# A normalised, quantised grouped convolution: TensorE's program as a loop of six trips over four images

## The chip, the cores and the metric

The kernel runs on one core of one Trainium2 chip. The metric is device time in microseconds (us) of one execution; the time before the change is a median of three runs. A profile is one execution, recorded instruction by instruction.

## The reference, cut to what matters

The input x is 32 images of 512 channels by 28 x 28 points (784), float32. Per image:

```python
x32 groups of 16 channels:  v = (x - mean) / sqrt(var + 1e-5)      # over 16 x 784 values
xg  = v as 4 groups of 128 channels, the groups rotated by one
xa  = round(clip((xg - lA) / (uA - lA), 0, 1) * 15) / 15
wq  = (round(clip((weight - lW) / (uW - lW), 0, 1) * 15) / 15 - 0.5) * 2
y   = einsum('bgihw,goi->bgohw', xa, wq)                           # 128 x 128 per group
y   = relu(y * inv + (beta - running_mean * inv))                  # inv = gamma / sqrt(running_var + 1e-5)
out = x + (y + v)
```

Every image is read once (1.6 MB) and written once (1.6 MB). Means and variances are of one image alone, so images can be worked on one behind the other.

## The kernel before, in words

All engines stream over the 32 images. Twelve image buffers (`images`, `RING`) hold an image as 128 channels of a partition group x 4 groups x 784. SyncE issues the loads (line 199); the load of image n waits until the store of image n-12 has landed. ScalarE issues 30 of the 32 stores (line 262), SyncE the last two (lines 203 and 212, the last one in four quarters).

Statistics of an image are taken five images ahead (`AHEAD`) by VectorE (`bn_stats`, line 460, summed in line 468 for a pair of images) and ScalarE (lines 236 and 242). TensorE averages them over 16 channels, for a pair u of images at a time: `average_means(u)` (lines 575 to 578), ScalarE copies the means (line 250), GpSimd makes the deviations (lines 375 to 382), `average_deviations(u)` (line 584) adds them up; then come a square root on ScalarE (line 257), a reciprocal on VectorE (line 492) and the coefficients on GpSimd (lines 398 to 406).

An image is then quantised to int16 `levels` (ScalarE line 270, mostly three groups; GpSimd line 424, the fourth), capped to bf16 `codes` by VectorE (`cap`, line 475), and multiplied by the weights, which are split in three bf16 parts: `multiply(n, g)` (lines 594 to 605) is six matmuls of 128 x 392, the last of which waits for GpSimd's in-place affine of the same group (line 413, semaphore `y_pool`). The sum goes to one of three PSUM sets of `prod`. VectorE's `finish(n, g)` (line 482) takes the set, applies the floor of the relu and adds it to the image; its semaphore `final` counts the sets that are free again and the groups that are done.

What sets the order: each engine's program is written out by hand and runs in that order; engines wait for each other by counting semaphores. TensorE's order for an odd image is multiply 0, 1, 2, `average_means`, multiply 3; for an even image `average_deviations`, multiply 0, 1, 2, 3. VectorE's for image n is finish 0, finish 1, cap(n+1), finish 2, half a group of statistics, finish 3, three more halves. With sets dealt in turn, `multiply` of the k-th group (k = 4n + g) waits for `finish` of group k-3:

```python
def multiply(n, g):
    k = G * n + g
    if g == 0:
        pe.wait_ge(capped, n + 1)
    if k >= SETS:
        pe.wait_ge(final, k - SETS + 1)
```

TensorE's program is unrolled: 999 matmuls with 999 weight loads.

Of the kernel before, what the change touches and what calls it, by code (L numbers as in the profile page):

```python
# [23 lines left out]
HELPED = 4  # L24
ACT_STORES = 30
SETS = 3
SUBSETS = 4
DMA = 16


def fused_norm_quantised_conv(nc, x, weight, limits, channel_params, out):

    B, C, H, W = x.shape
    G = CONV_GROUPS
    HW = H * W
    HALF = HW // 2
    PER_NORM = C // NORM_GROUPS
    COUNT = HW // SUBSETS
    PAIRS = B // 2
# [6 lines left out]
    def stats_on_dve(u):  # L46
        return 3 if u < 2 else 2
# [6 lines left out]
    def affine_on_act(n):  # L54
        return 2 if n >= B - HELPED else 0

    def y_pool_until(n):
        return sum(G - affine_on_act(i) for i in range(n + 1))

    def y_act_until(n):  # L60
        return sum(affine_on_act(i) for i in range(n + 1))
# [7 lines left out]
    def squares_until(u):  # L69
        return sum(2 * (G - stats_on_dve(i)) for i in range(u + 1))  # L70
# [7 lines left out]
    def output_group(g):  # L78
        return (g + G - 1) % G

    with ExitStack() as ctx:
        def sb(name, shape, dtype):
            return ctx.enter_context(nc.sbuf_tensor(name, shape, dtype))

        def ps(name, shape, dtype):
            return ctx.enter_context(nc.psum_tensor(name, shape, dtype))

        def sem(name):
            return ctx.enter_context(nc.semaphore(name))
# [3 lines left out]
        codes = sb("codes", [P, 2, G, HW], BF16)  # L93


        stats = sb("stats", [P, 2, 2, G, SUBSETS, 3], F32)
        sums = sb("sums", [P, 2, 2, 2, G], F32)
        unused = sb("unused", [P, 2, HW], BF16)
        gmean = sb("gmean", [P, 2, 2, G], F32)
        dev = sb("dev", [P, 2, G, SUBSETS], F32)  # L100
        dev2 = sb("dev2", [P, 2, G, SUBSETS], F32)
        half_var = sb("half_var", [P, 2 * G], F32)
# [15 lines left out]
        w_t = sb("w_t", [P, PARTS, G, P], BF16)  # L118
# [8 lines left out]
        floor = sb("floor", [P, G], F32)  # L127
# [6 lines left out]

        prod = ps("prod", [P, SETS, 2, 512], F32)
        mean_ps = ps("mean_ps", [P, 512], F32)
# [24 lines left out]
        squared = sem("squared")  # L161
# [3 lines left out]
        dev_done = sem("dev_done")  # L165
# [9 lines left out]
        y_pool = sem("y_pool")  # L175
        y_act = sem("y_act")
        final = sem("final")
# [151 lines left out]
        def _(pool):  # L329
            step = [0]  # L330

            def chained(ins):
# [21 lines left out]
                                            pattern=[[PER_NORM, P // PER_NORM], [0, PER_NORM]], channel_multiplier=-1))  # L354
            nc.gpsimd.tensor_scalar(avg[:], avg_one[:], 1.0 / SUBSETS, None, ALU.mult)
            nc.gpsimd.tensor_scalar(avg_n[:], avg_one[:], 1.0 / HW, None, ALU.mult).then_inc(consts_done, 1)
# [12 lines left out]
            def deviations(u):  # L369
                k, par = stats_on_dve(u), u % 2  # L370
                pool.wait_ge(gmean_done, u + 1)
                if u >= 1:
                    pool.wait_ge(var_done, u)
                mean = gmean[:, par].unsqueeze(3)
                nc.gpsimd.tensor_tensor(dev[:, :, 0:k], stats[:, par, :, 0:k, :, 1],  # L375
                                        mean[:, :, 0:k].to_broadcast([P, 2, k, SUBSETS]), ALU.subtract)
                own = sums[:, par, 0].unsqueeze(3)
# [67 lines left out]
        def _(dve):  # L445
# [31 lines left out]
            def finish(n, g):  # L477
                o = output_group(g)
                k = G * n + g
                dve.wait_ge(multiplied, k + 1)  # L480
                two = images[:, n % RING, o].rearrange("p (h f) -> p h f", h=2)
                nc.vector.scalar_tensor_tensor(out=two, in0=prod[:, k % SETS, :, 0:HALF], scalar=floor[:, o:o + 1],  # L482
                                               in1=two, op0=ALU.max, op1=ALU.add).then_inc(final, 1)

            def image_stats(n):
# [31 lines left out]
            for g in range(G):  # L517
                done = nc.vector.tensor_scalar(w_raw[:, g], w_rest[:, g], bn[:, 3, g:g + 1], None, ALU.mult)
# [18 lines left out]
            for n in range(B):  # L537
                m = n + AHEAD
                finish(n, 0)
                finish(n, 1)  # L540
                if n == 0:
                    rough_rstd(1)
                if n + 1 < B:
                    cap(n + 1)
                finish(n, 2)
                if m < B:
                    half_stats(m, 0, 0)
                finish(n, 3)
                if m < B:
                    half_stats(m, 0, 1)  # L550
                    half_stats(m, 1, 0)
                    half_stats(m, 1, 1)
                    if m % 2 == 1:
                        sum_stats(m // 2)
                if n % 2 == 1 and (n + 3) // 2 < PAIRS:
                    rough_rstd((n + 3) // 2)

        @block.tensor
        def _(pe):
            pe.wait_ge(consts_done, 1)  # L560
            pe.wait_ge(rows_in, DMA)
            nc.tensor.transpose(cols_ps[:, 0:4 * G], rows[:], ident[0:4 * G, 0:4 * G])
            pe.wait_ge(limits_in, DMA)
            nc.tensor.matmul(cols_ps[:, 4 * G:5 * G], one_row[:], limit_row[:], start=True,
                             stop=True).then_inc(cols_turned, 1)

            def average_means(u):
                k, par = stats_on_dve(u), u % 2
                pe.wait_ge(bn_summed, u + 1)
                pe.wait_ge(squared, squares_until(u))  # L570
                if u >= 1:
                    pe.wait_ge(gmean_done, u)
                    pe.wait_ge(std_done, u)
                mean = mean_ps[:, 0:2 * G].rearrange("p (j g) -> p j g", g=G)
                nc.tensor.matmul(mean[:, :, 0:k], avg[:], sums[:, par, 0, :, 0:k], start=True, stop=True)  # L575
                nc.tensor.matmul(mean[:, :, k:G], avg_one[:], sums[:, par, 0, :, k:G], start=True,  # L576
                                 stop=True).then_inc(mean_done, 1)
                nc.tensor.matmul(var_ps[:, 0:2 * G], avg_n[:], sums[:, par, 1], start=True, stop=False)

            def average_deviations(u):  # L580
                pe.wait_ge(dev_done, u + 1)
                var = var_ps[:, 0:2 * G].rearrange("p (j g) -> p j g", g=G)
                for s in range(SUBSETS):
                    done = nc.tensor.matmul(var, avg[:], dev2[:, :, :, s], start=False, stop=(s == SUBSETS - 1))  # L584
                done.then_inc(var_done, 1)


            def wait_affine(n, g):
                if g < G - affine_on_act(n):
                    pe.wait_ge(y_pool, (y_pool_until(n - 1) if n else 0) + g + 1)  # L590
                else:
                    pe.wait_ge(y_act, y_act_until(n - 1) + g - (G - affine_on_act(n)) + 1)

            def multiply(n, g):
                k = G * n + g
                if g == 0:
                    pe.wait_ge(capped, n + 1)
                if k >= SETS:
                    pe.wait_ge(final, k - SETS + 1)
                for part in range(PARTS):  # L600
                    for h in range(2):
                        if (part, h) == (PARTS - 1, 1):
                            wait_affine(n, g)
                        done = nc.tensor.matmul(prod[:, k % SETS, h, 0:HALF], w_t[:, part, output_group(g)],  # L604
                                                codes[:, n % 2, g, h * HALF:(h + 1) * HALF],
                                                start=(part == 0), stop=(part == PARTS - 1))
                done.then_inc(multiplied, 1)

            pe.wait_ge(w_scaled, 1)
            for g in range(G):  # L610
                turned = nc.tensor.transpose(prep_ps[:, g], w_raw[:, g], ident[:])
            turned.then_inc(w_turned, 1)
            average_means(0)
            average_deviations(0)
            pe.wait_ge(w_ready, 1)

            for n in range(-1, B - 1):
                if n < 0:
                    average_means(1)
                    multiply(0, 0)  # L620
                    average_deviations(1)
                    multiply(0, 1)
                    multiply(0, 2)
                else:
                    if n % 2 and (n + 3) // 2 < PAIRS:
                        average_deviations((n + 3) // 2)
                    multiply(n + 1, 0)
                    multiply(n + 1, 1)
                    multiply(n + 1, 2)
                    if n % 2 == 0 and (n + 4) // 2 < PAIRS:  # L630
                        average_means((n + 4) // 2)
                multiply(n + 1, 3)


_LIMITS = ["L0_conv_lW", "L0_conv_uW", "L0_conv_lA", "L0_conv_uA"]
# [20 lines left out]
```

## Time and profile before

| what | before |
|---|---|
| median of 3 runs | 259.03 us (258.69 to 259.69) |
| the profiled execution, its own time | 258.41 us |
| its span, first to last instruction | 256.7 us |
| VectorE / ScalarE / GpSimd / TensorE busy | 230.0 / 215.2 / 212.0 / 193.9 us |
| moved by DMA | 103.25 MB, mean 402 GB/s |
| mean granted clock of TensorE | 0.902 of full |

An engine's busy time is the time of its instructions; the rest of the span it waits or has no work. The DMA share is the mean over the core's 16 DMA engines, in which packets can overlap a little, so that full use reads as 1.03. A queue marked "instruction" carries an engine's own program code. The chain of waits is followed back from the last instruction. PE is TensorE, PEld its weight loads, DVE VectorE, ACT ScalarE, POOL GpSimd, SP SyncE.

### The profile page before, as it was taken

What the parts mean: (1) busy time and instruction counts of PE and PEld (TensorE: products, weight loads), DVE (VectorE), ACT (ScalarE), POOL (GpSimd) and SP (SyncE); (2) the same over time, 40 slices, a digit from 0 to 9 for tenths busy, and PEclk for the clock granted to TensorE, in tenths of its full rate; (3) what the DMA queues carried; (4) which work ended last, traced back from release to release, by engine and by line L of the source; (5) the groups of instructions that cost most, each with busy time, mean ns of one, the idle gap of its engine ahead of it and who ended that gap; (6) DMA issues with size and microseconds to landing.
All of it is one profiled execution on the core that took longest, in us unless ns stands there. A gap on an engine that the chain in (4) does not pass through costs nothing.

```text
span 256.7 us, 3463 instructions
## 1 busy us (share of the span) xinstructions
PE 193.9 (76%) x999; PEld 109.3 (43%) x999; DVE 230.0 (90%) x363; ACT 215.2 (84%) x394; POOL 212.0 (83%) x340
## 2 busy tenths in 40 slices
PE   1142996969889888979797997877696969889920
PEld 0132644435454444445443554343444435454510
DVE  2898698999999999999999899999999999969940
ACT  4437898999999999989999889999899888999300
POOL 6126869999999999999999999999999999999100
PEclk9999999797979798988979599999979797979995
DMA  6999999999999999999999999999999999999994
GB/s 225 398 411 411 408 409 406 418 416 417 418 414 418 417 416 418 411 418 416 416 415 416 418 416 413 419 417 415 417 413 418 416 418 409 402 400 402 393 399 193
DMA packets 34516, 103.25 MB, mean 402 GB/s; under 512 B 1202, under 2 KB 1730, under 8 KB 34498
## 3 DMA queue, kind: packets, MB, share of 16 engines
q1 hardware_dynamic: 18624, 54.86, 53.8%
q10 hardware_dynamic: 15874, 48.18, 47.0%
q8 instruction: 8, 0.13, 0.2%
q14 instruction: 10, 0.08, 0.1%
HBM read 51.65 MB, written 51.38 MB: 401 GB/s over the span
## 4 chain that ended last, share of the span: by engine, by line
POOL 52%; DVE 16%; issue 11%; PE 9%; ACT 5%; DMA 2%; DVEq 0%; SPq 0%; POOLq 0%; ACTq 0%
POOL images L413 27%; POOL levels L424 8%; DVE images L482 7%; PE prod L604 6%; DVE stats L460 4%; POOL dev L375 3%; DVE codes L475 3%; PE var_ps L584 3%; POOL dev L378 2%; DMA images<-in_x 2%; POOL scaled L404 2%; ACT levels L270 2%; POOL coef L406 2%; POOL norm L402 1%; ACT unused L242 1%
## 5 line engine op out<-in xcount | busy, mean ns | idle before, releaser
L604 PE MATMUL prod<-codes,w_t 128*128 128x392 bf16 x768 | 160.8, 369 | 7.9 <-DVE codes L475 2.9
L482 DVE SCALAR_TENSOR_TENSOR images<-prod,floor,images 128x784 f32<-128x784 f32 x128 | 128.0, 1019 | 8.5 <-PE prod L604 8.2
L413 POOL TENSOR_SCALAR images<-images,coef 128x784 f32<-128x784 f32 x120 | 123.7, 1042 | 0.0
L604 PEld LDWEIGHTS prod<-codes,w_t 128*128 128x128 bf16 x768 | 79.1, 110 | 81.6 <-issue 24.6
L270 ACT ACTIVATE levels<-images,coef 128x784 int16<-128x784 f32 x95 | 91.3, 1028 | 1.1 <-issue 1.1
L460 DVE BATCH_NORM_STATS2 stats<-images 128x6 f32<-128x392 f32 x136 | 68.9, 551 | 5.4 <-DMA images<-in_x 5.4
L236 ACT ACTIVATE unused<-images 128x784 bf16<-128x784 f32 x60 | 50.7, 847 | 7.5 <-DMA images<-in_x 5.2
L242 ACT ACTIVATE unused<-images,sums 128x784 bf16<-128x784 f32 x60 | 56.1, 939 | 0.1
L475 DVE TENSOR_SCALAR codes<-levels 128x3136 bf16<-128x3136 int16 x32 | 34.7, 1085 | 1.0 <-ACT levels L270 0.7
L584 PE MATMUL var_ps<-dev,avg 128*128 128x8 f32 x128 | 19.6, 280 | 20.0 <-POOL dev L382 20.0
L424 POOL TENSOR_SCALAR levels<-images,coef 128x784 int16<-128x784 f32 x33 | 33.6, 1020 | 0.1
L584 PEld LDWEIGHTS var_ps<-dev,avg 128*128 128x128 f32 x128 | 18.6, 221 | 25.4 <-POOL dev L382 25.2
L375 POOL TENSOR_TENSOR dev<-stats,gmean 128x16 f32<-128x16 f32 (+1 forms) x16 | 10.9, 682 | 9.6 <-ACT gmean L250 9.6
L575 PE MATMUL mean_ps<-sums,avg 128*128 128x4 f32 (+1 forms) x32 | 6.5, 274 | 12.2 <-DVE sums L468 12.2
L575 PEld LDWEIGHTS mean_ps<-sums,avg 128*128 128x128 f32 x32 | 5.2, 203 | 17.2 <-DVE sums L468 12.2
L242 ACT ACTIVATION_READ_ACCUMULATOR unused<-images,sums 128x1 f32 x60 | 11.4, 190 | 0.0
L236 ACT ACTIVATION_READ_ACCUMULATOR unused<-images 128x1 f32 x60 | 11.3, 188 | 0.0
L256 ACT ACTIVATE half_var<-var_ps,eps 128x8 f32<-128x8 f32 x16 | 4.2, 265 | 6.7 <-PE var_ps L584 6.4
L398 POOL TENSOR_TENSOR newt<-rough 128x8 f32<-128x8 f32 x16 | 3.9, 242 | 5.5 <-DVE rough L492 5.5
L250 ACT ACTIVATE gmean<-mean_ps 128x8 f32<-128x8 f32 x16 | 2.7, 170 | 6.1 <-PE mean_ps L576 6.0
L278 ACT ACTIVATE images<-images,coef 128x784 f32<-128x784 f32 x8 | 7.7, 1032 | 0.0
L404 POOL TENSOR_TENSOR scaled<-norm,coef_mul 128x32 f32<-128x32 f32 x16 | 6.5, 409 | 1.2
(66 smaller groups left out, 83.2 us busy)
## 6 DMA issues: line engine op xcount, KB each, us to landing
images<-in_x SPq DMA_DIRECT2D x30, 1568.0 KB, 14.5
out<-images ACTq DMA_DIRECT2D x30, 1568.0 KB, 18.8
images<-in_x SPq DMA_DIRECT2D x8, 392.0 KB, 6.6
out<-images SPq DMA_DIRECT2D x1, 1568.0 KB, 8.8
out<-images SPq DMA_DIRECT2D x4, 392.0 KB, 7.4
w_raw<-in_weight SPq DMA_DIRECT2D x1, 256.0 KB, 6.5
rows<-in_channel_params ACTq DMA_DIRECT2D x1, 8.0 KB, 2.3
limit_row<-in_limits ACTq DMA_DIRECT2D x1, 0.0 KB
```

The source lines that it names most:

```text
L236: nc.scalar.activation(unused[:, g % 2], images[:, n % RING, g], ACT.Identity, scale=1.0 / HW, accum_out=sums[:, u % 2, 0, j, g:g + 1]).th ...
L242: nc.scalar.activation(unused[:, g % 2], images[:, n % RING, g], ACT.Square, scale=-1.0, bias=sums[:, u % 2, 0, j, g:g + 1], accum_out=sum ...
L270: nc.scalar.activation(levels[:, n % 2, g], images[:, n % RING, g], ACT.Relu, bias=coef[:, u % 2, 1, 0, G * j + g:G * j + g + 1], scale=co ...
L375: nc.gpsimd.tensor_tensor(dev[:, :, 0:k], stats[:, par, :, 0:k, :, 1], mean[:, :, 0:k].to_broadcast([P, 2, k, SUBSETS]), ALU.subtract)
L413: nc.gpsimd.tensor_scalar(here, here, coef[:, u % 2, 0, 1, G * j + o:G * j + o + 1], coef[:, u % 2, 1, 1, G * j + o:G * j + o + 1], ALU.mu ...
L424: nc.gpsimd.tensor_scalar(levels[:, n % 2, g], images[:, n % RING, g], coef[:, u % 2, 0, 0, G * j + g:G * j + g + 1], coef[:, u % 2, 1, 0, ...
L460: nc.vector.bn_stats(two, images[:, n % RING, g, h * HALF:(h + 1) * HALF]).then_inc(bn_done, 1)
L475: nc.vector.tensor_scalar(codes[:, n % 2], levels[:, n % 2], 0.0, TOP, ALU.max, ALU.min).then_inc(capped, 1)
L482: nc.vector.scalar_tensor_tensor(out=two, in0=prod[:, k % SETS, :, 0:HALF], scalar=floor[:, o:o + 1], in1=two, op0=ALU.max, op1=ALU.add).t ...
L575: nc.tensor.matmul(mean[:, :, 0:k], avg[:], sums[:, par, 0, :, 0:k], start=True, stop=True)
L584: done = nc.tensor.matmul(var, avg[:], dev2[:, :, :, s], start=False, stop=(s == SUBSETS - 1))
L604: done = nc.tensor.matmul(prod[:, k % SETS, h, 0:HALF], w_t[:, part, output_group(g)], codes[:, n % 2, g, h * HALF:(h + 1) * HALF], start= ...
```

## The change

TensorE's program is no longer unrolled. Image 0 stands ahead of a loop; the loop `pe.Fori(0, 6)` has a body of four images (1 to 4 in trip 0, up to 21 to 24 in trip 5); images 25 to 31 are unrolled behind it. Counts to wait for are linear in the trip number `t` and are computed in registers. As a body of four images holds 16 groups, which three sets in turn would not divide, the sets are dealt by a table: an even image uses sets 0, 2, 1, 2 for its groups 0 to 3, an odd one 0, 1, 2, 1. `SET_LAST_USED` says how many groups back a set was last used: 4, 3, 3, 2 for groups 0 to 3. VectorE's `finish` reads by the same table. Nothing else is changed on VectorE, and nothing on ScalarE, GpSimd and SyncE.

```diff
+PSUM_SET = ((0, 2, 1, 2), (0, 1, 2, 1))
+SET_LAST_USED = (4, 3, 3, 2)
+BODY = 4
...
-                nc.vector.scalar_tensor_tensor(out=two, in0=prod[:, k % SETS, :, 0:HALF], scalar=floor[:, o:o + 1],
+                nc.vector.scalar_tensor_tensor(out=two, in0=prod[:, PSUM_SET[n % 2][g], :, 0:HALF], scalar=floor[:, o:o + 1],
...
-            def average_means(u):
-                k, par = stats_on_dve(u), u % 2
+            def average_means(t, v):
+                k, par = stats_on_dve(v), v % 2
+                u = BODY // 2 * t + v
                 pe.wait_ge(bn_summed, u + 1)
-                pe.wait_ge(squared, squares_until(u))
+                pe.wait_ge(squared, squares_until(v) + t * (squares_until(v + BODY // 2) - squares_until(v)))
...
-            def average_deviations(u):
-                pe.wait_ge(dev_done, u + 1)
+            def average_deviations(t, v):
+                pe.wait_ge(dev_done, BODY // 2 * t + v + 1)
...
-            def multiply(n, g):
-                k = G * n + g
+            def multiply(t, i, g):
+                n = BODY * t + i
                 if g == 0:
                     pe.wait_ge(capped, n + 1)
-                if k >= SETS:
-                    pe.wait_ge(final, k - SETS + 1)
+                if G * i + g >= SET_LAST_USED[g]:
+                    pe.wait_ge(final, G * n + g - SET_LAST_USED[g] + 1)
...
+            def image_products(t, i, more):
+                if more and i % 2 == 0:
+                    average_deviations(t, (i + 2) // 2)
+                for g in range(G - 1):
+                    multiply(t, i, g)
+                if more and i % 2 == 1:
+                    average_means(t, (i + 3) // 2)
+                multiply(t, i, G - 1)
...
+            chained_images = B - 8
+            assert chained_images % BODY == 0 and chained_images < B - HELPED
+            with pe.Fori(0, chained_images // BODY) as t:
+                for i in range(1, 1 + BODY):
+                    image_products(t, i, True)
+            for n in range(1 + chained_images, B):
+                image_products(0, n, (n + 2) // 2 < PAIRS if n % 2 == 0 else (n + 3) // 2 < PAIRS)
```

The first place is TensorE from the end of an odd image (its means, its group 3) to the start of the even one that follows. Before, with the semaphores that a row waits for in brackets:

```order
L575 MATMUL mean_ps<-sums,avg 128x2x2 [waits gmean_done,std_done,squared,bn_summed]
L576 MATMUL mean_ps<-sums,avg_one 128x2x2
L578 MATMUL var_ps<-sums,avg_n 128x8
L604 MATMUL prod<-codes,w_t 128x392 [waits final]
L604 MATMUL prod<-codes,w_t 128x392 x4
L604 MATMUL prod<-codes,w_t 128x392 [waits y_pool]
L584 MATMUL var_ps<-dev,avg 128x8 [waits dev_done]
L584 MATMUL var_ps<-dev,avg 128x8 x3
L604 MATMUL prod<-codes,w_t 128x392 [waits final,capped]
```

The same place with the change, in the loop's body:

```order
L576 ISA [waits bn_summed]
L578 REGISTER_ALU [waits squared]
L581 MATMUL mean_ps<-sums,avg 128x2x2 [waits std_done,gmean_done]
L582 MATMUL mean_ps<-sums,avg_one 128x2x2
L584 MATMUL var_ps<-sums,avg_n 128x8
L612 MATMUL prod<-codes,w_t 128x392 [waits final]
L612 MATMUL prod<-codes,w_t 128x392 x4
L596 REGISTER_ALU
L612 MATMUL prod<-codes,w_t 128x392 [waits y_pool]
L590 MATMUL var_ps<-dev,avg 128x8 [waits dev_done]
L605 REGISTER_ALU
L607 ISA [waits capped]
```

The matmuls stand in the same order. Register instructions stand between them, and the waits for `bn_summed`, `squared` and `capped` have moved from a matmul to an instruction of the sequencer ahead of it. The second place is the end of the body, where the last group of an even image is followed by the way back:

```order
L612 MATMUL prod<-codes,w_t 128x392 [waits final]
L612 MATMUL prod<-codes,w_t 128x392 x4
L596 REGISTER_ALU
L612 MATMUL prod<-codes,w_t 128x392 [waits y_pool]
L642 REGISTER_ALU
L642 COMPARE_AND_BRANCH
```

Before, the first matmul of the next (odd) image stood there; now that matmul is the body's first, behind a branch.

## Rows read from the trace of the kernel before

**Rows 1.** The page: busy time, share, instructions; the DMA share in 40 slices.
```profile
PE 193.9 (76%) x999; PEld 109.3 (43%) x999; DVE 230.0 (90%) x363; ACT 215.2 (84%) x394; POOL 212.0 (83%) x340
DMA  6999999999999999999999999999999999999994
```

**Rows 2.** Windows: stretch, its us, busy (instructions) per engine, PE clock, DMA share, GB/s.
```profile
100.00:120.00 20.00, 18.11 (x90) 9.63 (x90) 19.05 (x31) 19.17 (x40) 18.98 (x32) 0.83 1.03 415
248.00:250.00 2.00, 0.00 (x0) 0.00 (x0) 0.00 (x0) 0.00 (x0) 0.00 (x0) 1.00 1.03 401
252.00:252.50 0.50, 0.00 (x0) 0.00 (x0) 0.00 (x0) 0.00 (x0) 0.00 (x0) 0.50 0.84 326
253.00:253.50 0.50, 0.00 (x0) 0.00 (x0) 0.00 (x0) 0.00 (x0) 0.00 (x0) 0.50 0.53 207
255.00:255.50 0.50, 0.00 (x0) 0.00 (x0) 0.00 (x0) 0.00 (x0) 0.00 (x0) 0.50 0.05 19
```

**Rows 3.** Timeline of the end: start, us, engine, line, tiles.
```profile
241.20 5.73 DVE L482 SCALAR_TENSOR_TENSOR images<-prod,floor,images 128x784 f32<-128x784 f32 x6
...
244.13 4.31 SPq L212 DMA_DIRECT2D out<-images  x4
```

**Rows 4.** DMA issues by line: how many, KB each, median us from issue to landing.
```profile
images<-in_x SPq DMA_DIRECT2D x30, 1568.0 KB, 14.5
...
out<-images SPq DMA_DIRECT2D x4, 392.0 KB, 7.4
...
rows<-in_channel_params ACTq DMA_DIRECT2D x1, 8.0 KB, 2.3
```

**Rows 5.** The code queue over the whole span: packets, MB, share of 16 engines.
```profile
q8 instruction: 8, 0.13, 0.2%
```

**Rows 6.** The code queue alone, in the stretch 210 to 240 us.
```profile
q8 instruction: 2, 0.03, 0.4%
```

**Rows 7.** Windows, columns as in rows 2, for TensorE's count of instructions.
```profile
0.00:43.00 43.00, 20.50 (x89) 13.68 (x89) 32.41 (x68) 29.23 (x56) 24.95 (x61) 1.00 0.98 380
43.00:75.00 32.00, 27.26 (x143) 15.35 (x144) 31.88 (x51) 29.93 (x60) 30.82 (x47) 0.86 1.03 417
```

**Rows 8.** Timeline of TensorE around the turn from an odd to an even image.
```profile
110.02 0.39 PE L575 MATMUL mean_ps<-sums,avg 128*128 128x4 f32 x2 [0.53 <-DVE sums L468]
...
110.96 1.17 PE L604 MATMUL prod<-codes,w_t 128*128 128x392 bf16 x6
113.18 1.21 PE L584 MATMUL var_ps<-dev,avg 128*128 128x8 f32 x8 [1.05 <-POOL dev L382]
114.24 9.21 PE L604 MATMUL prod<-codes,w_t 128*128 128x392 bf16 x42
123.97 0.39 PE L575 MATMUL mean_ps<-sums,avg 128*128 128x4 f32 x2 [0.53 <-DVE sums L468]
```

**Rows 9.** Timeline of VectorE over the same pair of images.
```profile
109.88 1.96 DVE L482 SCALAR_TENSOR_TENSOR images<-prod,floor,images 128x784 f32<-128x784 f32 x2
111.76 0.97 DVE L475 TENSOR_SCALAR codes<-levels 128x3136 bf16<-128x3136 int16 x1
...
114.07 1.01 DVE L482 SCALAR_TENSOR_TENSOR images<-prod,floor,images 128x784 f32<-128x784 f32 x1
...
117.95 1.03 DVE L482 SCALAR_TENSOR_TENSOR images<-prod,floor,images 128x784 f32<-128x784 f32 x1 [0.45 <-PE prod L604]
118.90 0.97 DVE L475 TENSOR_SCALAR codes<-levels 128x3136 bf16<-128x3136 int16 x1
```

**Rows 10.** Timeline: the copy of the means, and the deviations of this pair and the next.
```profile
110.66 0.18 ACT L250 ACTIVATE gmean<-mean_ps 128x8 f32<-128x8 f32 x1 [0.60 <-PE mean_ps L576]
...
112.89 0.24 POOL L382 TENSOR_TENSOR dev<-dev 128x32 f32<-128x32 f32 x1
...
125.61 0.21 POOL L375 TENSOR_TENSOR dev<-stats,gmean 128x16 f32<-128x16 f32 x1
```

**Rows 11.** Windows, columns as in rows 2, TensorE's clock behind the same turn.
```profile
114.24:117.10 2.86, 2.86 (x10) 1.31 (x11) 2.86 (x6) 2.72 (x9) 2.86 (x4) 0.50 1.04 417
```

More of the change, by code:

```diff
@@ L565, in _ @@
                              stop=True).then_inc(cols_turned, 1)
-            def average_means(u):
-                k, par = stats_on_dve(u), u % 2
+            def average_means(t, v):
+                k, par = stats_on_dve(v), v % 2
+                u = BODY // 2 * t + v
                 pe.wait_ge(bn_summed, u + 1)
-                pe.wait_ge(squared, squares_until(u))
-                if u >= 1:
+                pe.wait_ge(squared, squares_until(v) + t * (squares_until(v + BODY // 2) - squares_until(v)))
+                if v >= 1:
                     pe.wait_ge(gmean_done, u)
@@ L585, in average_deviations, with wait_affine @@
                 done.then_inc(var_done, 1)
-            def wait_affine(n, g):
-                if g < G - affine_on_act(n):
-                    pe.wait_ge(y_pool, (y_pool_until(n - 1) if n else 0) + g + 1)
-                else:
-                    pe.wait_ge(y_act, y_act_until(n - 1) + g - (G - affine_on_act(n)) + 1)
-            def multiply(n, g):
-                k = G * n + g
+            def wait_affine(n, i, g):
+                if i < B - HELPED:
+                    pe.wait_ge(y_pool, G * n + g + 1)
+                elif g < G - affine_on_act(i):
+                    pe.wait_ge(y_pool, y_pool_until(i - 1) + g + 1)
+                else:
+                    pe.wait_ge(y_act, y_act_until(i - 1) + g - (G - affine_on_act(i)) + 1)
+            def multiply(t, i, g):
+                n = BODY * t + i
                 if g == 0:
                     pe.wait_ge(capped, n + 1)
-                if k >= SETS:
-                    pe.wait_ge(final, k - SETS + 1)
+                if G * i + g >= SET_LAST_USED[g]:
+                    pe.wait_ge(final, G * n + g - SET_LAST_USED[g] + 1)
                 for part in range(PARTS):
@@ L602, in multiply @@
                         if (part, h) == (PARTS - 1, 1):
-                            wait_affine(n, g)
-                        done = nc.tensor.matmul(prod[:, k % SETS, h, 0:HALF], w_t[:, part, output_group(g)],
-                                                codes[:, n % 2, g, h * HALF:(h + 1) * HALF],
+                            wait_affine(n, i, g)
+                        done = nc.tensor.matmul(prod[:, PSUM_SET[i % 2][g], h, 0:HALF], w_t[:, part, output_group(g)],
+                                                codes[:, i % 2, g, h * HALF:(h + 1) * HALF],
                                                 start=(part == 0), stop=(part == PARTS - 1))
                 done.then_inc(multiplied, 1)
+            def image_products(t, i, more):
[6 more added lines that the diff above has]
+                multiply(t, i, G - 1)
             pe.wait_ge(w_scaled, 1)
@@ L612, in _ @@
             turned.then_inc(w_turned, 1)
-            average_means(0)
-            average_deviations(0)
+            average_means(0, 0)
+            average_deviations(0, 0)
             pe.wait_ge(w_ready, 1)
[L617 to L632, printed above, removed]
+            average_means(0, 1)
+            multiply(0, 0, 0)
+            average_deviations(0, 1)
+            for g in range(1, G):
+                multiply(0, 0, g)
+            chained_images = B - 8
[5 more added lines that the diff above has]
+                image_products(0, n, (n + 2) // 2 < PAIRS if n % 2 == 0 else (n + 3) // 2 < PAIRS)
 _LIMITS = ["L0_conv_lW", "L0_conv_uW", "L0_conv_lA", "L0_conv_uA"]
```

## The prediction, made before the changed kernel ran

> **What bounds the kernel now.** I read the page's first two parts first. VectorE, the busiest engine, is at 90%, TensorE at 76%, but the DMA share stands at 9 in all slices but the first and the last [rows 1]. The windows say it in numbers: 1.03 of the 16 DMA engines at 415 GB/s in the middle, with VectorE at 19.05 of 20 us and GpSimd at 18.98 [rows 2]. So two limits run side by side, the transfers and the engines, and the end tells which one closes the run. VectorE's last finish ends at 246.9 us, and the last quarter of the last store is issued by 248.4 [rows 3]. After that no engine works, and the DMA engines are still full at 250 us; then they fall idle one after another, 0.84 busy at 252, 0.53 at 253, 0.05 at 255 [rows 2]. The transfers close the run; the engines are ahead of them by the backlog at that moment. Its size: a 392 KB quarter lands 7.4 us after its issue; an 8 KB transfer into empty queues took 2.3 us, and 392 KB at 401 GB/s are 1.0 us more, so without backlog it would take an estimated 3.3 us [rows 2, 4]. **The engines' cushion is 7.4 - 3.3 = 4.1 us**: engine work may end that much later before the run does.
>
> **The change, part by part.** Against the profiled execution, 258.41 us (span 256.7 and 1.7 around it), which is 0.6 below the median of 259.03.
>
> *Removed: program code.* The unrolled program has 999 matmuls and 999 weight loads, and the queue that carries 16 KB pieces of code brought 8 of them, 0.13 MB [rows 1, 5]. That is TensorE's: 0.13 MB over 1998 instructions is 65 bytes each, so a piece is some 256 instructions, and TensorE starts 143 + 144 in 32 us [rows 7], 256 in 28.5, about as often as pieces come. Two pieces in 30 us took 0.4% of 16 engines, or 0.96 us of one engine each [rows 6]. The rewritten program has some 835 instructions (59 matmuls ahead of the loop, 124 in its body, 168 + 42 behind it, each with its load, and about 50 others), so if every piece came once, some 5 fewer would be fetched: 5 x 0.96 / 16 = 0.3 us less DMA work per engine.
>
> *Added: the way back.* Five times a branch jumps back over the body, 124 matmuls, 124 loads and 35 others, about 283 instructions, more than one piece. By 43 us TensorE had started 89 + 89 instructions, and the first piece was not fetched until about then [rows 7]: with those queued ahead, that is the step into the second piece. So the fetcher seems to hold the piece in use and the next, and the body's first piece would be gone when the branch is reached. Then each of five ways back fetches it again, with one or two pieces behind it: 10 to 15 fetches in place of the 5 or 6 that these images had, net 5 to 10 more, +0.3 to +0.6 us per DMA engine. I take that: **+0.4 us**; the other end is -0.3.
>
> How long does such a fetch hold TensorE? No row shows one. Below: 0.96 us for the piece itself. Above: 14.5 us, what a load of 1568 KB takes through the full queues [rows 4, 6]. What hides it: TensorE's sequencer runs ahead of the engine. The 178 instructions started at the first fetch, against 256 in a piece, say by some 60 and more. The body ends behind an even image. Its codes are capped at 112.7, its 48 instructions start on the engine at 114.24 behind the 16 for the deviations, and the next odd image can't start before its own codes at 118.90 + 0.97 = 119.87 [rows 8, 9]. With 64 ahead the branch is passed at about 114.3: 5.6 us of cover. Behind that, the odd image's group 2 may end 1.3 us later until the means reach GpSimd too late (TensorE idles 0.53 ahead of the means; the copy behind them ended at 110.84, 13.95 later is 124.79, and GpSimd's deviations start at 125.61, another 0.8) [rows 8, 10]. Cover is **about 6.9 us**; I take a stall nearer to the small transfers, 3 to 6 us, since it is one packet on one engine and not 32 on each: nothing exposed.
>
> The Trainium skill (Runtime: NRT & Kernel Launch, Instruction fetch mechanics) has a rule that speaks against the change: a taken branch whose target is outside the two pages held forces a fetch before execution goes on, and so it calls unrolling preferable where possible. By it each of the five ways back stalls the sequencer; it gives no time for that, and by my cover the sum stays as it is unless one takes over 6.9 us. That only one piece at a time comes in agrees with the trace [rows 5]; that a branch stalls, no row here shows.
>
> *Moved: who waits for which set.* Group 0 now waits for a finish four back, earlier than before; groups 1 and 2 as before; group 3 two back, that is finish 1 of its own image in place of finish 0. For the odd image: finish 0 ends at about 110.9 and TensorE started group 3 at 110.96; finish 1 ends at 111.84, so it starts 0.9 us later and ends at about 113.05 [rows 8, 9]. Who is behind it: VectorE's finish 3, which begins at 114.07, and the deviations' matmuls, which can't start before 113.13 when GpSimd is done [rows 9, 10]. Both are covered, the second by 0.1 us. These six took 1.17 us, full clock (2.4 GHz); it is at the lower of its two levels from 114.24 to 117.10, behind TensorE's idle 1.05 us [rows 8, 11], where group 3 is not. For the even image: finish 1 ends at 118.98, and group 3 starts by its own pace at about 119.0. No loss. Taken: **0 us**; the other end is 0.9 us in each of 12 pairs, 11 us of engine time.
>
> *Added: waits and sums on the sequencer.* 35 rows per body. The waits for `capped`, `bn_summed` and `squared` now hold the sequencer, so behind each the first load is issued after the event and not released by it. Bounds: 0, and 0.2 us at each of 6 such places per body, an estimate: twice the 0.1 us that now pass between the end of finish 0 and the matmul at 110.96 [rows 8, 9]. The odd image's group 0 and its means have the 1.3 and 0.8 us from above. Taken: 0.
>
> Sum: 258.41 + 0.4 + 0 + 0 = 258.8, or on the median's scale 259.03 + 0.4: **259.4 us**.
>
> **The rivals.** About 0.5% (1.3 us) is what a measurement of this kernel can tell from no change.
>
> *A fetch behind the branch outlasts its cover (slower).* One mechanism, at the start of images 5, 9, 13, 17, 21, deciding from 6.9 us. At 9 us, 2.1 x 5 = 10.5 us of engine time less the cushion of 4.1 give +6.4: 265.4; at the 14.5 of a load 5 x 7.6 - 4.1 = 34: 293. For: the queues are full. Against: the fetches of straight code never show, and it is one packet. 0.08.
>
> *The code comes in on DMA engines that are late already (slower).* Landing is by the slowest of 16. The engines end between 252 and 255.5 [rows 2]. Ten more pieces, 9.6 us, if all on the last engine: 268; half of them on it, +4.8: 263.8; on engines that end early: nothing. 0.08.
>
> *The new set wait or the sequencer's waits lengthen every pair (slower).* 0.1 us of cover is thin. At 0.5 us in 12 pairs 6 - 4.1 = +1.9: 260.9; at 0.9 +6.7: 265.7. 0.06.
>
> *The pieces are kept, and their absence relieves the last DMA engine (faster).* Five fewer, 4.8 us on the engine that ends last; then the others set the end, between 253 and 254 in place of 255.5: 257.2. 0.08.
>
> *The change doesn't do what it says.* The order of the new program has a compare and branch and one body; excluded.
>
> **How the numbers follow.** No measurable change takes the rest: 0.70 (258.7 to 259.8, by whether pieces are kept). Slower 0.08 + 0.08 + 0.06 = 0.22, faster 0.08. The range goes from 258.0 to 262.5: it holds the forecast with its bounds, and of the slower cases those with a small price; left out are the faster case and somewhat over half of the slower ones.
>
> **What would show it.** Right: DMA share 1.03 until about 252, VectorE's last finish before 251, the odd image's group 3 0.9 us later behind finish 1, 13 to 18 pieces on the code queue, TensorE starting odd images within 0.2 us of their codes. Wrong: one idle stretch of several us on TensorE every four images with "issue" as its end, pairs longer than 13.96 us (from 110.02 to 123.97 for the means [rows 8]) in the chain of waits, DMA share falling before 252, or a tail longer than from 252 to 255.5.

## The result, and the profile after

Over 16 runs each, the changed kernel has a median of 261.44 us against 259.0 before. The ratios in this document leave out executions that took over 1.5% longer than the fastest of their kernel, here three of the changed kernel's 16; so taken, the ratio is 1.0084, with a 95% interval of 1.0065 to 1.0104. The change costs some 2.2 us, or 2.4 by the medians of all runs, beyond what could pass for no change. The likeliest case of the prediction, no measurable change at 0.70, did not come; its range of 258.0 to 262.5 holds the time. The profiled execution took 263.59 us, 2.2 above the median, so its idle times are on the large side. The unrolled kernels e1 and e3 below show the same lengthened pairs (a pair of images is the unit in which means and deviations are worked out) in executions of 261.09 us, e1's median, and 261.39, 0.7 below e3's.

The page of the changed kernel: engines, then the granted clock and the DMA share in 40 slices, and the queue that brings TensorE's code.

```profile
PE 205.9 (79%) x999; PEld 118.3 (45%) x999; DVE 230.7 (88%) x363; ACT 215.4 (82%) x394; POOL 212.9 (81%) x340
...
PEclk9999998686968779797958689797979596898997
DMA  6999999999999999999999999999999999867798
...
q8 instruction: 3, 0.05, 0.1%
```

Beside [rows 1], TensorE is busy 12 us more with the same 999 matmuls, since it runs them more often at the lower of its two clock levels, and the DMA share now leaves 9 before the end, in slices 35 to 38. The windows place that (columns as in rows 2):

```profile
0.00:220.00 220.00, 174.71 (x839) 101.59 (x839) 198.59 (x323) 190.23 (x357) 188.81 (x306) 0.85 1.02 409
220.00:240.00 20.00, 17.95 (x87) 9.71 (x88) 16.54 (x25) 16.78 (x29) 17.07 (x30) 0.81 0.84 329
240.00:250.00 10.00, 8.93 (x54) 4.82 (x53) 10.00 (x12) 8.38 (x9) 7.01 (x6) 1.00 0.68 264
```

Up to 220 us the transfers are full as before. Between 220 and 250 they starve: 0.84 and 0.68 where 1.03 is full, (1.03 - 0.84) x 20 + (1.03 - 0.68) x 10 = 7.3 us of it lost, because the engines no longer deliver finished images in time. VectorE's last finish ends at 255.9, 9 us later than in [rows 3].

Where the engines lose their time shows in what TensorE waited for (us in total, times, longest), first after the change and then before:

```profile
PE prod L612 <- DVE images L486: 13.2, 17, 1.1
...
PE var_ps L590 <- POOL dev L386: 3.5, 2, 2.0
```

```profile
PE var_ps L584 <- POOL dev L382: 20.0, 14, 2.3
...
PE prod L604 <- DVE images L482: 1.7, 4, 1.2
```

Before, the products waited for a set of `prod` 1.7 us in all, and the deviations' matmuls 20.0 us for GpSimd. Now the products wait 13.2 us for a set, and the deviations' matmuls only 3.5: the idle time has moved to the other side of group 3, and the deviations, ready long before, wait for TensorE. The timeline of one turn, to be read beside [rows 8] and [rows 9]:

```profile
85.36 1.97 DVE L486 SCALAR_TENSOR_TENSOR images<-prod,floor,images 128x784 f32<-128x784 f32 x2
85.68 0.35 PE L581 MATMUL mean_ps<-sums,avg 128*128 128x4 f32 x2 [0.58 <-DVE sums L472]
...
87.03 0.24 POOL L386 TENSOR_TENSOR dev<-dev 128x32 f32<-128x32 f32 x1
...
87.38 1.77 PE L612 MATMUL prod<-codes,w_t 128*128 128x392 bf16 x6 [0.90 <-DVE images L486]
...
88.94 1.72 PE L590 MATMUL var_ps<-dev,avg 128*128 128x8 f32 x8
...
90.51 6.38 PE L612 MATMUL prod<-codes,w_t 128*128 128x392 bf16 x24
...
92.67 1.03 DVE L486 SCALAR_TENSOR_TENSOR images<-prod,floor,images 128x784 f32<-128x784 f32 x1 [0.59 <-PE prod L612]
...
94.63 1.03 DVE L486 SCALAR_TENSOR_TENSOR images<-prod,floor,images 128x784 f32<-128x784 f32 x1 [0.93 <-PE prod L612]
95.58 1.35 DVE L479 TENSOR_SCALAR codes<-levels 128x3136 bf16<-128x3136 int16 x1
```

Finish 1 of the odd image ends at 87.33, and 0.05 us later TensorE starts group 3, as the new wait says. The deviations have been ready since 87.27. TensorE has idled 0.90 us, and its clock falls while group 3 runs; windows over group 3, the deviations and the first products of the even image:

```profile
87.38:89.15 1.77, 1.77 (x8) 1.14 (x8) 1.77 (x3) 1.77 (x5) 1.77 (x2) 0.62 1.04 418
89.15:90.66 1.51, 1.51 (x10) 1.47 (x9) 1.51 (x4) 0.86 (x3) 1.51 (x2) 0.50 1.03 413
90.66:94.70 4.04, 4.04 (x14) 1.83 (x13) 2.52 (x6) 3.91 (x10) 3.42 (x10) 0.51 1.04 418
```

Group 3, the deviations and most of the even image's products run at the lower level, and VectorE waits 0.59 and 0.93 us for the products. From the end of the odd image's finish 1 to the start of the even image's finish 1 it is 94.63 - 87.33 = 7.3 us; before it was 117.95 - 111.84 = 6.1 [rows 9], although the clock was at the lower level for a while there too. GpSimd's first deviation instruction marks the pairs; the first two lines are the pair just shown, the last two the same step of e5, which is described below:

```profile
86.56 0.22 POOL L379 TENSOR_TENSOR dev<-stats,gmean 128x16 f32<-128x16 f32 x1 [0.38 <-ACT gmean L254]
102.19 0.22 POOL L379 TENSOR_TENSOR dev<-stats,gmean 128x16 f32<-128x16 f32 x1 [1.45 <-ACT gmean L254]
```

```profile
83.81 0.99 POOL L379 TENSOR_TENSOR dev<-stats,gmean 128x16 f32<-128x16 f32 x1
97.85 1.00 POOL L379 TENSOR_TENSOR dev<-stats,gmean 128x16 f32<-128x16 f32 x1
```

The changed kernel's pair took 15.63 us, and GpSimd, which came to this step without waiting in [rows 10], waited 1.45 for the means. From one pair's means to the next it was 13.95 in [rows 8]. Not every pair is like this one. Of the 13 pairs whose deviations begin between 42 and 217 us four took 15.5 to 15.7 us, and these are the four whose group 3 took 1.7 to 2.1 us, that is, ran at the lower level for much of its time. In the other nine it took 1.17, as before, and the pairs took 13.95 to 14.5.

### The profile page after: what moved, and what is told of

It is laid out like the page before. It is cut to its first block, busy times and chain, and to the rows that moved or that the text cites. A ratio compares the mean times of both kernels' runs of the same rounds, so it can differ in the third digit from the quotient of the medians.

```text
span 261.9 us, 3638 instructions
## 1 busy us (share of the span) xinstructions
PE 205.9 (79%) x999; PEld 118.3 (45%) x999; DVE 230.7 (88%) x363; ACT 215.4 (82%) x394; POOL 212.9 (81%) x340
## 4 chain that ended last, share of the span: by engine, by line
DVE 34%; PE 33%; POOL 14%; issue 12%; DMA 2%; ACT 2%; ACTq 0%; SPq 0%; POOLq 0%; DVEq 0%
PE prod L612 24%; DVE images L486 15%; DVE stats L464 10%; PE var_ps L590 8%; POOL images L417 7%; DVE codes L479 7%; POOL levels L428 3%; DMA images<-in_x 2%; ACT levels L274 1%; POOL dev L382 1%; DVE sums L472 1%; POOL dev L379 1%; POOL dev L386 1%; PE mean_ps L581 1%; POOL newt L402 1%
## 5 line engine op out<-in xcount | busy, mean ns | idle before, releaser
L612 PE MATMUL prod<-codes,w_t 128*128 128x392 bf16 x768 | 170.0, 384 | 17.8 <-DVE images L486 13.2
L417 POOL TENSOR_SCALAR images<-images,coef 128x784 f32<-128x784 f32 x120 | 135.0, 1135 | 0.0
L612 PEld LDWEIGHTS prod<-codes,w_t 128*128 128x128 bf16 x768 | 83.0, 115 | 95.8 <-issue 35.4
L590 PEld LDWEIGHTS var_ps<-dev,avg 128*128 128x128 f32 x128 | 24.6, 277 | 7.6 <-POOL dev L386 6.5
L590 PE MATMUL var_ps<-dev,avg 128*128 128x8 f32 x128 | 23.8, 314 | 4.0 <-POOL dev L386 3.5
L379 POOL TENSOR_TENSOR dev<-stats,gmean 128x16 f32<-128x16 f32 (+1 forms) x16 | 5.0, 315 | 16.0 <-ACT gmean L254 16.0
L382 POOL TENSOR_TENSOR dev<-sums,gmean 128x16 f32<-128x16 f32 (+1 forms) x16 | 7.8, 490 | 0.0
```

The source lines that it names most:

```text
L382: nc.gpsimd.tensor_tensor(dev[:, :, k:G], own[:, :, k:G].to_broadcast([P, 2, G - k, SUBSETS]), mean[:, :, k:G].to_broadcast([P, 2, G - k, ...
L417: nc.gpsimd.tensor_scalar(here, here, coef[:, u % 2, 0, 1, G * j + o:G * j + o + 1], coef[:, u % 2, 1, 1, G * j + o:G * j + o + 1], ALU.mu ...
L612: done = nc.tensor.matmul(prod[:, PSUM_SET[i % 2][g], h, 0:HALF], w_t[:, part, output_group(g)], codes[:, i % 2, g, h * HALF:(h + 1) * HAL ...
```

## The experiments

Ten kernels, with 10 to 12 executions each, but six each for e1 and e3, whose intervals are wider. The ratio is that of the kernel to the kernel before on the same chip, with its 95% interval; the clock is TensorE's mean granted clock in the profiled execution. Three theories stand against each other: S blames the wait of group 3 for its set, L the loop's waits and register work, and C a clock that falls by the order in which the loop issues, whatever the sets.

**e1: the sets alone.** The kernel before, unrolled, with the new table.

```diff
+PSUM_SET = ((0, 2, 1, 2), (0, 1, 2, 1))
+SET_LAST_USED = (4, 3, 3, 2)
...
-                if k >= SETS:
-                    pe.wait_ge(final, k - SETS + 1)
+                if k >= SET_LAST_USED[g]:
+                    pe.wait_ge(final, k - SET_LAST_USED[g] + 1)
...
```

> The program stays unrolled; only the sets are dealt by the table (group 3 waits two groups back, group 0 four). Theory S (the set wait of group 3 makes the pairs longer, and TensorE's low clock goes with it): as slow as the change, ratio 1.006 to 1.011, mean granted clock 0.85 to 0.89, the DMA share under 1.0 in some 20 us stretch before 240 us. Theory L (the loop's waits and register work in the sequencer do it): ratio 1.000 within 0.002, clock 0.90. Theory C (the clock falls more often by the loop's issue pattern, whatever the sets): 1.000 as well.

Measured: 261.09 us, ratio 1.0088 (1.0055 to 1.0122), clock 0.879. The whole loss is there without any loop.

**e2: the loop alone.** The changed kernel with a body of 12 images (48 groups, which three sets in turn divide), two trips.

```diff
-BODY = 4
+BODY = 12
...
-                if G * i + g >= SET_LAST_USED[g]:
-                    pe.wait_ge(final, G * n + g - SET_LAST_USED[g] + 1)
+                if G * i + g >= SETS:
+                    pe.wait_ge(final, G * n + g - SETS + 1)
...
```

> The loop stays, with a body of 12 images and two trips, in which three sets in turn divide evenly; every wait for a set is three groups back as before. Theory S: ratio 0.998 to 1.002 and clock 0.90. Theory L: 1.006 to 1.011, since all waits of the sequencer are still there, 35 rows for every four images. One way back in place of five: if the branch costs, at most a fifth of it is left.

Measured: 259.25 us, ratio 1.0014 (0.9999 to 1.0028), clock 0.897. The sequencer's waits do show in the timeline. This is the turn from VectorE's sum to the matmuls of the means in e2, and then in the kernel before:

```profile
96.17 0.26 DVE L472 TENSOR_REDUCE sums<-stats 128x4 f32<-128x16 f32 x2
...
96.67 0.36 PE L581 MATMUL mean_ps<-sums,avg 128*128 128x4 f32 x2 [0.50 <-DVE sums L472]
```

```profile
95.74 0.26 DVE L468 TENSOR_REDUCE sums<-stats 128x4 f32<-128x16 f32 x2
...
96.05 0.39 PE L575 MATMUL mean_ps<-sums,avg 128*128 128x4 f32 x2 [0.53 <-DVE sums L468]
```

From the end of the sum to the first matmul it is 96.67 - 96.43 = 0.24 us against 96.05 - 96.00 = 0.05. So a wait that is held by the sequencer costs about 0.2 us more; in the run's time that is not to be told from nothing.

**e3 and e4: which of the two waits.** Before, with sets in turn, and only one count raised, for odd images (e3, as below) or for even ones (e4, `(0, 3)`). No set changes its place, so nothing but the wait differs.

```diff
-                    pe.wait_ge(final, k - SETS + 1)
+                    pe.wait_ge(final, k - (2 if (n % 2, g) == (1, 3) else SETS) + 1)
```

> Before, with sets in turn, and one count raised: group 3 of odd images waits two groups back (finish 1 of its own image). Theory S with the odd image as the place (group 3 starts 0.9 us later, the deviations' matmuls stand behind it): 1.005 to 1.010. If the even image is the place: 1.000 within 0.002.

> The same, for group 3 of even images alone. Theory S with the odd image as the place: 1.000 within 0.002, since group 3 of the even image starts about when finish 1 ends. If both count: each 1.002 to 1.006.

Measured: e3 262.12 us, 1.0119 (1.0086 to 1.0152), clock 0.879; e4 258.93 us, 1.0002 (0.9987 to 1.0017), clock 0.897. The odd image's wait is all of it. In e3 (waits on TensorE) the products' waits have grown as in the changed kernel:

```profile
PE prod L604 <- DVE images L482: 17.7, 26, 1.1
...
PE var_ps L584 <- POOL dev L382: 4.2, 4, 1.5
```

And e3's pairs differ among themselves, by GpSimd's first deviation instruction of each; below them is group 3 on TensorE in the second and in the third of these pairs:

```profile
98.96 0.21 POOL L375 TENSOR_TENSOR dev<-stats,gmean 128x16 f32<-128x16 f32 x1
112.91 0.21 POOL L375 TENSOR_TENSOR dev<-stats,gmean 128x16 f32<-128x16 f32 x1
127.06 0.22 POOL L375 TENSOR_TENSOR dev<-stats,gmean 128x16 f32<-128x16 f32 x1 [0.25 <-ACT gmean L250]
142.57 0.22 POOL L375 TENSOR_TENSOR dev<-stats,gmean 128x16 f32<-128x16 f32 x1 [1.22 <-ACT gmean L250]
```

```profile
113.18 1.17 PE L604 MATMUL prod<-codes,w_t 128*128 128x392 bf16 x6 [1.05 <-DVE images L482]
...
128.03 1.86 PE L604 MATMUL prod<-codes,w_t 128*128 128x392 bf16 x6 [1.05 <-DVE images L482]
```

The pairs took 13.95, 14.15 and 15.51 us. TensorE idles the same 1.05 us ahead of group 3 in each, and some lose nothing; the pair that loses is the one in which group 3 ran at the lower level. That pointed to the clock, and to e5.

**e5: the wait stays, the idle time is filled.** The changed kernel with four extra matmuls behind the means of odd images, into columns of `var_ps` that nothing reads.

```diff
+            def keep_busy(count, j):
+                for _ in range(count):
+                    nc.tensor.matmul(var_ps[:, 64:64 + HALF], w_t[:, 0, 0], codes[:, j, 0, 0:HALF], start=False, stop=False)
...
                     average_means(t, (i + 3) // 2)
+                    keep_busy(4, i % 2)
```

> The change, and four extra 128 x 392 matmuls behind the means of every odd image, where TensorE idles some 0.9 us for finish 1 (they add products that nothing reads into unused columns of var_ps). If the low clock is what turns the 0.9 us into lost time: mean granted clock 0.92 or more, ratio to before 1.000 to 1.003. If the wait alone costs and the clock only follows: clock higher, ratio still 1.006 or more. If idle time there is not what lowers the clock: clock under 0.90 and ratio 1.006 to 1.012.

Measured: 258.69 us, ratio 0.999 (0.9979 to 1.0001), clock 0.971. The same turn as above:

```profile
95.70 0.36 PE L581 MATMUL mean_ps<-sums,avg 128*128 128x4 f32 x2 [0.31 <-DVE sums L472]
...
96.36 0.82 PE L619 MATMUL var_ps<-codes,w_t 128*128 128x392 bf16 x4
97.31 1.17 PE L612 MATMUL prod<-codes,w_t 128*128 128x392 bf16 x6
99.39 1.06 PE L590 MATMUL var_ps<-dev,avg 128*128 128x8 f32 x8 [0.92 <-POOL dev L386]
```

Group 3 still starts only at 97.31, behind finish 1, but takes 1.17 us, and the deviations' matmuls again wait for GpSimd and not the reverse. The pair took 14.04 us. The wait by itself costs nothing at the full clock; it costs where it lets the clock fall. One of its 12 executions took 304.21 us at a mean clock of 0.608; whether the filling has to do with that is not settled.

**e6: the tight reuse moved.** The changed kernel, loop and all, with the sets dealt so that the reuse after two groups lies on group 0.

```diff
-PSUM_SET = ((0, 2, 1, 2), (0, 1, 2, 1))
-SET_LAST_USED = (4, 3, 3, 2)
+PSUM_SET = ((2, 0, 1, 2), (1, 0, 2, 1))
+SET_LAST_USED = (2, 4, 3, 3)
```

> The change with another deal of the three sets over two images (even 2, 0, 1, 2; odd 1, 0, 2, 1): the reuse after two groups lies on group 0, the one after four on group 1. Loop of six trips and all its waits as in the change. If the place of the tight reuse decides: group 0 waits for finish 2 of the image before, which ends 0.9 us behind the codes for an odd image and before TensorE is free for an even one, so ratio 0.999 to 1.004. If any reuse after two groups costs as much: 1.006 to 1.011. If the five ways back cost anything of their own, it is left here: ratio above 1.003 with idle time at images 5, 9, 13, 17, 21.

Measured: 258.91 us, ratio 0.9999 (0.9986 to 1.0012), clock 0.903. This keeps the loop and gives the loss back. At image 5, the body's first in trip 1, VectorE's finish 2 of image 4 and then TensorE:

```profile
65.00 1.03 DVE L486 SCALAR_TENSOR_TENSOR images<-prod,floor,images 128x784 f32<-128x784 f32 x1
```

```profile
66.09 3.16 PE L612 MATMUL prod<-codes,w_t 128*128 128x392 bf16 x18 [1.60 <-DVE images L486]
```

The finish ends at 66.03, and the first matmul behind the branch starts 0.06 us later. By itself this shows only that no stall outlasted the 1.60 us that TensorE waited here. The sequencer's own rows in the changed kernel tell more: first the branch over all six trips (duration least, median, most in ns; first and last start in us), then the end of trip 0 alone.

```profile
L642 PEldq COMPARE_BRANCH  x6: 83/215/233, 65.8 to 210.7; - x6
```

```profile
L642 PEldq COMPARE_BRANCH  x1: 233/233/233, 65.8 to 65.8; - x1
L642 PEldq FUSED_REGOPS  x1: 50/50/50, 66.1 to 66.1; - x1
```

The five branches that were taken took 0.22 to 0.23 us each, and the one that was not took 0.08. The register instruction at the body's top starts right behind: there is no stall.

**e7 and e9: how far the end can slip.** Before, with 16 (e7) or 36 (e9) extra matmuls ahead of the products of image 31.

```diff
+                if (n, g) == (B - 1, 0):
+                    keep_busy(16, n % 2)
```

> Before, with 16 extra 128 x 392 matmuls ahead of the products of image 31 (into unused columns of mean_ps, read by nothing): 16 x 0.195 = 3.1 us at the full clock. Measures the cushion of the engines. If it is 4.1 us, as forecast: VectorE ends some 2.6 to 3.1 us later and the ratio is 1.000 within 0.003. If the cushion is nothing: +2.6 us or more, 1.010.

> As with 16 extra matmuls ahead of the products of image 31, with 36 of them, 36 x 0.195 = 7.0 us. With 16, VectorE's last finish ended at 250.0 in place of 246.9 and the time stayed. If the cushion is 4.1 us: last finish at about 253.9, and 253.9 + the forecast's 3.3 us for the last quarter and some 3 us behind it give a ratio of 1.008 to 1.015. If it is larger (6 us or more): under 1.004.

Measured: e7 259.06 us, 1.0004 (0.9991 to 1.0017); e9 259.19 us, 1.0001 (0.9985 to 1.0017). The last finishes and the issues of the last stores in e9:

```profile
249.02 4.02 DVE L482 SCALAR_TENSOR_TENSOR images<-prod,floor,images 128x784 f32<-128x784 f32 x4 [5.35 <-PE prod L610]
250.09 3.32 SPq L212 DMA_DIRECT2D out<-images  x4
```

VectorE ends at 253.0, 6.1 us later than in [rows 3], the last quarter is issued at 253.4, 5.0 us later, and no time is lost that could be told from nothing. The last quarters landed 3.2 us after issue in the median (7.4 in [rows 4]), close to the 3.3 that was estimated for a transfer without backlog, and the DMA share from 250 to 251 is down to 0.21. So this is about as late as the end can be. Yet e1, whose VectorE ends at 252.4, earlier than that, is slower by 2 us. Its windows say why:

```profile
220.00:230.00 10.00, 8.15 (x46) 4.26 (x44) 9.51 (x15) 9.05 (x15) 9.45 (x17) 0.98 1.02 395
230.00:240.00 10.00, 9.82 (x50) 5.53 (x50) 7.92 (x10) 8.50 (x11) 9.23 (x15) 0.83 0.78 305
240.00:250.00 10.00, 8.53 (x50) 4.53 (x48) 10.00 (x12) 4.96 (x6) 3.49 (x3) 1.00 0.89 349
```

A single late image at the end meets a backlog of stores. A delay that has built up over the whole run makes the backlog run out between 230 and 240, some 20 us before the end, and what the DMA engines miss there does not come back.

**e8 and e10: does a full clock gain anything?** e8 is the kernel before with five extra matmuls ahead of the deviations; e10 is e6 with three behind the means.

> Before, with five extra matmuls of the same kind ahead of the deviations' matmuls, where TensorE idles 1.05 us per pair. If transfers close the run: clock 0.95 or more, VectorE's end earlier by some us, ratio 0.998 to 1.001. If the low clock of TensorE costs time before as well: 0.995 or less.

> The loop with the tight reuse on group 0 and three extra matmuls behind the means of odd images: both remedies together, to see whether anything beats the kernel before. If transfers close the run: ratio 0.997 to 1.001, clock 0.95 or more, VectorE's last finish before 247. If a version with the engines well ahead still gains: under 0.997.

Measured: e8 258.87 us, 0.9994 (0.9982 to 1.0007), clock 0.979; e10 259.07 us, 1.0001 (0.9989 to 1.0012), clock 0.946. The clock rises and the time stays, and no version beat the kernel before. But the last finishes did not come as early as was expected: e8's ends at 246.4, 0.5 us earlier than in [rows 3] where some us were expected, and e10's at 248.6, not before 247. Nearly all of e8's pairs take 14.05 us, about as long as before, so a faster TensorE doesn't speed up the other engines. The two runs show that a fuller clock gains nothing here; as a test of whether the transfers close the run they are weak.

## Why the prediction was right or wrong

**The time lies in the range, but not by the sum.** The sum said 259.4 and no measurable change. That 261.44 lies within 258.0 to 262.5 is owed to the upper end, which was set for slower cases with a small price, weighed at 0.22 together; as far as the mechanism goes it is luck. Two of the text's own signs of being wrong came: pairs longer than 13.96 us, and a DMA share that falls before 252.

**What bounds the kernel: right.** Transfers close the run before the change (e9: VectorE's end 6.1 us later, no loss), and for a loss the engines have to fall behind them, which they did.

**"Taken: 0 us" for who waits for which set: this is the step that failed.** The 0.9 us of delay was right (0.90 us idle ahead of group 3), and so was the even image's "no loss" (e4). Wrong was "Both are covered, the second by 0.1 us", and behind it the sentence that the clock is low only "where group 3 is not". Group 3's time was taken at the full clock, as it was before, in a place where the change itself puts 0.9 us of idle time ahead of it. With the clock at the lower level six matmuls took 1.77 us, the deviations waited 1.7 us for TensorE (87.27 to 88.94), and much of the rest of the pair ran low. Mean clock 0.90 before, 0.85 to 0.894 in the changed kernel's executions; e3 has the loss from this wait alone, e5 takes it away by filling the idle time. The text had a rival at this place, with 0.06, at 260.9 for 0.5 us in each of 12 pairs. The place was right, and the weight far too low for a cover it called thin itself. The mechanism was not: it had a little lost in every pair for want of cover, while four of 13 pairs lost 1.6 to 1.7 us each because the clock had fallen, and the others 0.5 or less. That its price came within 0.6 us of the median is in part chance.

**The cushion of 4.1 us: mis-sized, and read at the wrong place.** For a delay of the last image alone it is about 6 us (e9). Some 1.1 us of that is not in the backlog: before, the last quarter was issued 1.5 us behind VectorE's last finish [rows 3], in e9 0.4 us. For a delay that has built up over all images it is smaller: GpSimd's deviation step of the last pair but one (u = 14) started at 209.9 us before, at 211.9 in e4 without loss, and at 214.5 in e1 with one of 2 us; so it lies between 2.0 and 4.6 us at that point. The last load is issued at about 201 us; that the place to read the cushion is behind it, where only stores are left, fits the windows of e1, but no run tests it.

**"+0.4 us" for code fetched again: wrong.** Three pieces came in, not 13 to 18, and none between 50 and 215 us, where all five ways back lie (65.8 to 181.9). Even e2, with a body of some 850 instructions, over three pieces, fetched 5 in all, and none between 100 and 205 us, though the body ran a second time from 118.7 to 202.9. What the body needs stays where it is. With that the rival of code that comes in on late DMA engines falls too (its 268 is on the profiled execution's scale; on the median's it would be 268.6). The five fewer pieces gave nothing to see either (e6: 0.9999), so the faster rival had no footing.

**The branch: right that it costs nothing, but not by its cover.** There was no stall to hide. The cover of 6.9 us was wrong: it had the sequencer 64 instructions ahead and the branch passed 5.6 us before the next codes. In the changed kernel the first way back started at 65.8, while the first matmuls of the last group ran, and the codes of image 5 were ready at 66.8, so some 0.8 us are left behind the branch; a stall of 3 to 6 us would have shown. The Trainium skill (Runtime: NRT & Kernel Launch, Instruction fetch mechanics) gives TensorE room for 2048 instructions, and its warning is of a target outside the two pages held. The traces agree with the first, since no program here had a piece fetched twice; that only two pages of 256 are held isn't what TensorE shows in e2.

**The sequencer's waits: right.** 0.24 us from the event to the matmul at the means, 0.19 more than before and so at the upper bound given, 0.15 at the codes of image 5, and absorbed (e2).

## What to carry to other kernels

A wait that fits under the cover of the trace before can still cost, if the idle time that it makes lets TensorE's clock fall: price what runs behind new idle time at the lower level, as a bound at least. When few buffers are dealt to a loop that they don't divide, some reuse is tighter than before; choose which one by the timeline, since the same table rotated by one group was free here and the other cost 0.8%. And how far engines may fall behind saturated transfers can't be read at the last instruction alone: look also where the backlog is smallest.

## What the runs showed of the hardware that was not expected

- TensorE's code in a loop was not fetched again: 3 pieces of 16 KB with five ways back over some 283 instructions (8 for the unrolled program), 5 for a body of 12 images.
- A taken compare and branch of TensorE's sequencer took 0.22 to 0.23 us, one not taken 0.08. The first matmul behind the branch started 0.06 us after the finish it waited for (e6). A wait held by the sequencer ahead of a matmul, in place of one at the matmul, took 0.24 us from the event to the start, not 0.05.
- Idle time of 0.9 to 1.05 us ahead of group 3 was enough to lower the mean granted clock from 0.90 to 0.88 (e3). Four or five matmuls per pair of images that fill idle time brought it to 0.97 (e5) and 0.98 (e8).
- The last quarter stores of 392 KB landed in 3.2 us (median) in e9, where the DMA share had fallen to 0.21 as they were issued, against 7.4 behind a backlog.
